# Half of the one-hot matrices on ScalarE, one joint inverse root, a shorter ELU, mixer columns from DRAM and the bias at an eviction

## The reference, cut to what matters

```python
def _rgcn_layer(X, W, root, bias, gamma, beta, src, dst, etype, inv_deg):
    h = jnp.einsum('ni,rio->rno', X, W)
    msg = h[etype, src] * inv_deg[:, None]
    agg = jax.ops.segment_sum(msg, dst, num_segments=X.shape[0])
    out = agg + X @ root + bias
    mu = jnp.mean(out, axis=-1, keepdims=True)
    var = jnp.mean(jnp.square(out - mu), axis=-1, keepdims=True)
    out = (out - mu) * jax.lax.rsqrt(var + EPS) * gamma + beta
    out = jax.nn.elu(out)
    return out + X
...
# the mixer beside it (elu(q)+1, elu(k)+1, a sum over all nodes, two layer norms, a gelu layer)
t = jnp.einsum('nlhd,nhmd,nlh->nlhm', q, kv, z)
x1 = layer_norm(t + x, ln1_g, ln1_b)
h = jax.nn.gelu(jnp.einsum('nfc,oc->nfo', x1, W1) + b1, approximate=False)
y = jnp.einsum('nfc,oc->nfo', h, W2) + b2
return layer_norm(y + x1, ln2_g, ln2_b)
```

## Time and profile before

| | us |
|---|---|
| median of 3 runs | 8429.41 (8418.92 to 8451.86) |
| the profiled execution | 8445.94, its span 8444.1 |
| VectorE busy | 4887.0 (58% of the span) |
| TensorE busy | 5985.2 (71%) |
| ScalarE busy | 1584.5 (19%) |
| GpSimd busy | 4238.0 (50%) |

### The profile page before, as it was taken

The page is one execution under the profiler, slowest core; times in us unless marked ns, Lnnn a source line. Parts: engine busy times, 40 slices in busy tenths (PEclk is TensorE's granted clock), DMA queues, the critical chain, the costliest instruction groups (busy, mean ns, idle before and its releaser), DMA issues. The chain is left out here.

```text
span 8444.1 us, 107673 instructions
## 1 busy us (share of the span) xinstructions
PE 5985.2 (71%) x18474; PEld 3592.9 (43%) x18474; DVE 4887.0 (58%) x16836; ACT 1584.5 (19%) x3834; POOL 4238.0 (50%) x4288
## 2 busy tenths in 40 slices
PE   0587777767777767777776777778488677664398
PEld 0244444444544444444443333345334444443265
DVE  7106666667777767777776677732433666662412
ACT  0231112211111113333330000022021111110132
POOL 0007677756666656666656777710000777762211
PEclk9799899988788888889887666679699888877699
DMA  1324444433333333434434333300034333330000
GB/s 54 127 93 124 120 125 124 125 118 113 112 112 114 113 117 114 118 116 119 119 111 127 104 104 104 103 24 0 0 129 138 105 105 105 105 92 2 12 14 17
DMA packets 457906, 797.23 MB, mean 94 GB/s; under 512 B 87260, under 2 KB 322100, under 8 KB 457609
## 3 DMA queue, kind: packets, MB, share of 16 engines
q0 software_dynamic: 200480, 548.02, 22.9%
q1 hardware_dynamic: 257382, 248.75, 8.9%
HBM read 606.70 MB, written 189.74 MB: 94 GB/s over the span
## 5 line engine op out<-in xcount | busy, mean ns | idle before, releaser
L515 POOL DMA_INDIRECT gnn_msg<-tables,gnn_row_ring x4165 | 4015.2, 964 | 2346.5 <-issue 1644.2
L559 PE MATMUL bank<-gnn_msg,gnn_hot 128*128 128x256 f32 x8330 | 3142.9, 496 | 1292.5 <-DVE sums L544 1030.5
L559 PEld LDWEIGHTS bank<-gnn_msg,gnn_hot 128*128 128x128 f32 x8330 | 1715.7, 235 | 2586.6 <-DVE sums L544 1928.3
L544 DVE TENSOR_TENSOR sums<-sums,bank 128x256 f32 x4165 | 1746.5, 419 | 1587.6 <-PE bank L559 1127.2
L524 DVE TENSOR_SCALAR gnn_hot<-iota,gnn_meta_ring 128x128 f32<-128x128 f32 x3332 | 1127.5, 356 | 332.0 <-ACT gnn_meta_ring L508 332.0
L133 POOL TENSOR_TENSOR ve<-mv,eps 128x7 f32<-128x7 f32 x35 | 7.2, 205 | 1348.3 <-DVE mv L127 1199.7
L652 PE MATMUL bank<-gnn_w,residual 128*128 128x512 f32 x1176 | 572.5, 611 | 1.4 <-ACT residual L668 1.4
L507 ACT COPY gnn_row_ring<-row 128x9 int32 (+1 forms) x490 | 97.8, 200 | 1512.7 <-PE bank L559 1498.8
L1698 PE MATMUL bank<-tables_w,sums 128*128 128x512 f32 x784 | 338.3, 593 | 6.4 <-ACTq L117 6.4
L652 PEld LDWEIGHTS bank<-gnn_w,residual 128*128 128x128 f32 x1176 | 237.2, 202 | 174.7 <-issue 152.9
L672 ACT COPY residual<-bank 128x512 f32<-128x512 f32 x294 | 172.3, 586 | 681.3 <-PE bank L652 681.3
(11 more groups left out here) (398 smaller groups left out, 6804.7 us busy)
## 6 DMA issues: line engine op xcount, KB each, us to landing
tables<-residual SPq DMA_DIRECT2D x294, 256.0 KB, 2.7
gnn_msg<-tables,gnn_row_ring POOLq DMA_INDIRECT x4165, 2.8
tables<-sums SPq DMA_DIRECT2D x98, 512.0 KB, 2.9
tables<-gnn_msg SPq DMA_DIRECT2D x98, 256.0 KB, 2.1
residual<-first_norm SPq DMA_DIRECT2D x98, 128.0 KB, 3.1
first_norm<-state SPq DMA_DIRECT2D x1, 6272.0 KB, 20.8
first_rows<-residual SPq DMA_DIRECT2D x1, 6272.0 KB, 39.0
mixer_rows<-residual SPq DMA_DIRECT2D x49, 128.0 KB, 2.4
```

The lines of the kernel that those rows point to most:

```text
L515: self.nc.gpsimd.indirect_dma_start(out=self.msg[:, s0 + u, :], out_offset=None, in_=table, in_offset=bass.IndirectOffsetOnAxis(ap=self.ro ...
L544: self.nc.vector.tensor_tensor(at, at, self.sums(s), ALU.add).then_inc(self.added, 1)
L559: self.nc.tensor.matmul(self.sums(s), self.hot[:, s, :], self.msg[:, s, :], start=True, stop=True).then_inc(self.summed, 1)
```

## The change

Five things are changed in `gnn0` and its helpers, the first one in `gnn1` too.

1. **One-hots.** Of the 9 and 8 one-hots of a tile's halves VectorE makes 5 and 4. The last four of each half are made by ScalarE inside `ring`, right behind the two copies: four distances |place - iota|, a negated copy of the weights, then four max(weight - weight * distance, 0). So `ring` grows by nine instructions on ScalarE, and TensorE waits for these slots on a semaphore of their own.
2. **Joint root.** `Attend` and `Feed` no longer take an inverse root of their own behind their statistics. Their variance stands beside `Post`'s, and the root after slot 1 is taken of both columns at once, with 12 instructions in place of 9. The mixer's shift follows there, and ScalarE's `norm` moves to the start of its turn, ahead of the copy of the turned tile and of `Gelu` or `Exp`. `Keys0` and the fourth layer take the 12-instruction form for one column.
3. **ELU.** exp(min(u, 0)) takes a `Relu` and an `Exp` on ScalarE; VectorE's cut (L617) is gone, and the -1 goes into the addition to the state, which moves from slot 8 to slot 7.
4. **Mixer columns.** In the table stage the turned tiles are stored to DRAM (28 more DMAs); `Keys0` and `Attend` load them and neither transpose nor copy. `Feed` still does.
5. **Bias.** The one-row matmul is gone. VectorE adds the bias when it evicts the root product, in the table stage and after slot 15 of `Post`; ScalarE's copies of it are gone. `Post`'s steps on TensorE move one slot ahead (9, 11, 12, 14).

```diff
-NEXT_HOTS = (((), (0,), (1,), (2,), (3,), (4,), (5,), (6,), (7,)),
-             ((), (), (0, 1), (2,), (3,), (4, 5), (6,), (7, 8)))
+DVE_HOTS = (5, 4)
+ACT_HOTS = 4
+NEXT_HOTS = (((), (), (0,), (), (1,), (), (2,), (), (3,)),
+             ((), (), (0,), (1,), (), (2,), (3,), (4,)))
...
     def ring(self, act, i, n, h):
...
+        for k in range(ACT_HOTS):
+            u = DVE_HOTS[h] + k
+            self.nc.scalar.activation(self.away[:, k, :], self.c.iota[:], ACT.Abs, bias=m[:, u, 0:1], scale=-1.0)\
+                .then_inc(self.away_ready, 1)
+        if self.weighted:
+            self.nc.scalar.mul(m[:, :, 2], m[:, :, 1], -1.0).then_inc(self.away_ready, 1)
...
+        for k in range(ACT_HOTS):
+            u = DVE_HOTS[h] + k
+            to = self.hot[:, s0 + u, :]
+            if self.weighted:
+                ins = self.nc.scalar.activation(to, self.away[:, k, :], ACT.Relu, bias=m[:, u, 1:2], scale=m[:, u, 2:3])
...
     def vector(self, dve, n, t, cols, last=False):
...
-                inverse_root(dve, c, self.rs, self.half, self.tmp, self.mv[:, 1:2], self.s_root, n - 1)
+                inverse_root(dve, c, self.rs[:, 0:cols], self.half[:, 0:cols], self.tmp[:, 0:cols], self.mv[:, 0:cols, 1],
+                             self.s_root, n - 1)
...
             if s == 6:
                 dve.wait_ge(self.s_exp, n)
-                v.tensor_scalar(self.ex, self.ex, 1.0, -1.0, ALU.min, ALU.add).then_inc(self.s_cut, 1)
+                v.scalar_tensor_tensor(self.u, self.u, 0.0, self.ex, ALU.max, ALU.add).then_inc(self.s_elu, 1)
             if s == 7:
-                dve.wait_ge(self.s_cut, n)
-                v.scalar_tensor_tensor(self.u, self.u, 0.0, self.ex, ALU.max, ALU.add).then_inc(self.s_elu, 1)
-            if s == 8:
                 dve.wait_ge(self.s_elu, n)
...
-                    v.tensor_tensor(self.xs, state, self.u, ALU.add).then_inc(self.s_new, 1)
+                    v.scalar_tensor_tensor(self.xs, self.u, -1.0, state, ALU.add, ALU.add).then_inc(self.s_new, 1)
+            if s == 15 and not last:
+                dve.wait_ge(self.s_prod, n * 3)
+                v.tensor_tensor(agg, c.bank[1][:, 0:D], self.vecs[:, 2, :], ALU.add).then_inc(self.s_base, 1)
...
-        self.nc.scalar.activation(self.ex, self.u, ACT.Exp).then_inc(self.s_exp, 1)
+        self.nc.scalar.activation(self.ex, self.u, ACT.Relu, scale=-1.0).then_inc(self.s_neg, 1)
+        act.wait_ge(self.s_neg, n)
+        gate(act, self.c)
+        self.nc.scalar.activation(self.ex, self.ex, ACT.Exp, scale=-1.0).then_inc(self.s_exp, 1)
...
     def end_first(self, dve, i):
...
-        inverse_root(dve, c, self.rs, self.ve, self.tmp, self.mv[:, 1:2], self.s_pow, i)
-        v.scalar_tensor_tensor(self.shift, self.mv[:, 0:1], -1.0, self.rs, ALU.mult, ALU.mult).then_inc(self.s_rs, 1)
+
+    def shift_mean(self, dve):
+        self.nc.vector.scalar_tensor_tensor(self.shift, self.mv[:, 0:1], -1.0, self.rs, ALU.mult, ALU.mult).then_inc(self.s_rs, 1)
...
     def sync(self, sp, i, first, second):
         if first:
-            sp.wait_ge(self.s_turned, i + 1)
-            sp.dma_start(self.x, self.c.xn_d[ds(i * P, P), :]).then_inc(self.s_x, 16)
+            sp.wait_ge(self.s_mm, i + 1)
+            sp.dma_start(self.xt.rearrange("p h r -> p (h r)"), tile_columns(self.c, i)).then_inc(self.s_xt, 16)
...
-                            if j == 2:
-                                ins = nc.tensor.matmul(c.bank[b][:, 0:D], c.ones[0:1, :], brow[:], start=False, stop=True)
...
-                        nc.scalar.copy(tile_of(c.agg, g, k), c.bank[b][:, 0:D]).then_inc(s_root, 1)
...
+                with dve.Fori(0, NG) as g:
+                    for k in range(GT):
+                        b, t = turn(3 * k + 2, g)
+                        dve.wait_ge(c.bank_full[b], t)
+                        nc.vector.tensor_tensor(tile_of(c.agg, g, k), c.bank[b][:, 0:D], vecs[:, 2, :], ALU.add).then_inc(s_root, 1)
```

More of the change, by code:

```diff
@@ L531, in begin_vector @@
         dve.wait_ge(self.ring_ready, n * 4 + 2)
-        for u in range(HALF):
+        for u in range(DVE_HOTS[0]):
             self.one_hot(0, u)
@@ L932, in after @@
         def after(s):
-            if s == 6 and first:
+            if s == 1 and second:
+                self.shift_mean(dve)
+            if s == 5 and first:
                 dve.wait_ge(self.s_act, i * 2 + 3)
@@ L1029, in scalar @@
         c, sc = self.c, self.nc.scalar
+        if second:
+            self.norm(act, i)
         if first:
```

256 lines of the change are left out of this document (132 added, 124 removed).

## The result

| | us |
|---|---|
| kernel before, 4 runs | 8439.37 (8418.92 to 8451.86) |
| changed kernel, 4 runs | 8295.55 (8290.02 to 8312.18) |
| ratio | 0.9835 [0.9809, 0.9862] |
| profiled execution after | 8290.0, its span 8288.2 |

The change gained 144 us. The prediction said 324 (8105 us, range 7900 to 8270): right in sign, more than twice too much in size, and the range missed by 26 us.

A forecast was written before the change was run, and what follows sets the result against it. It took VectorE to bound Attend and Feed, TensorE Keys0's second half, and POOL's gathers the fourth layer and gnn1. -152 - 118 - 15 - 39 = -324 us from 8429.4 gave 8105 us, range 7900 to 8270.

The forecast's parts named there:

- Attend, -152: Layer beside Attend: VectorE's work falls 3.1 us a tile, 26.45 to 23.3, over 49 tiles -152 us.
- Feed, -118: Layer beside Feed: -2.85 us a tile on VectorE, +0.45 for ScalarE's order, so -2.4 a tile, -118 us.
- I take +0.45 for this stall and the later additions: Feed's tile: Exp ready at about 10.1 us, VectorE wanting it at 9.4; with later additions, 0.45 us a tile lost.
- Covered, with 1.2 us to spare: Attend's tile: despite the later turned tile, TensorE finishes slot 16 at 19.0 us, before VectorE's addition at 20.2.
- Keys0, -15: Layer beside Keys0: turned tile 1.0 us later, products and bias saving more; -0.3 a tile, -15 us.
- ScalarE's price, 3.3 us a half: ScalarE between ring copies and turned tile: eight instructions at 0.35 us, plus overlap and waits, 3.3 us a half.
- Table stage, -39: Table stage: no bias on TensorE -30 us, no root-product copy on ScalarE -9, stores of turned tiles 0.
- Fourth layer and gnn1, 0: These two layers stand at POOL's floor of back-to-back gathers, so no change, 0 us (-10 to +10).
- Rival 1: First three layers all reach the 21.4 us floor because VectorE's register loads hide: 7792 us, half-way about 7950; chance 0.18.
- Rival 2: ScalarE's chain 1 us longer a half: Keys0 and Feed lose 1 us a tile, Attend 0.5; 8227 us, chance 0.14.
- Rivals 3 and 4: 3: ScalarE between ring and turned tile, slower, 8600 us, chance 0.05. 4: TensorE's lower clock cancels layer savings, 8390, chance 0.05.
- Rival 5: Fewer VectorE one-hots free GpSimd's port in the two floor layers, 266 us more gained: 7839 us, chance 0.02.

The follow-up runs named there:

- norm_behind_c: Changed kernel with Feed's normalisation on ScalarE put back behind the turned tile's copy and Gelu: 8146.65 us, 0.9658 of the kernel before.
- norm_and_split_c: Changed kernel, Feed's normalisation behind copy and Gelu, half 0's ScalarE one-hots in two pieces behind the copy of Post's turned tile: 7982.26 us, 0.9468 of the kernel before.
- paced_vector: Changed kernel with all 17 one-hots on VectorE, POOL writing zeros instead of gathering in the first four layers: 8231 us, against 8285 with ScalarE's one-hots.
- narrow_before: Kernel before with each gather taking 32 numbers a row in place of 256, on a slow chip: 9785 us beside 9784 uncut.
- paced_elu: Changed kernel with the ELU of before, POOL writing zeros instead of gathering in the first four layers, on a slow chip: 8828 us.

## Why the prediction was wrong, point by point

- **Attend, -152:** right, -142, but part of the agreement is luck. The root did what was said: additions 11 and 12 stand 3.23 us apart, predicted 2.9 and before 5.6. The aggregation's wait shows with 0.30, not 0.15:

```profile
2426.40 0.42 DVE L551 TENSOR_TENSOR sums<-sums,bank 128x256 f32 x1 [0.21 <-DVE sums L551]
...
2429.63 0.42 DVE L551 TENSOR_TENSOR sums<-sums,bank 128x256 f32 x1 [0.30 <-DVE gnn_own L834]
```

  A joint step takes 0.59 us (predicted 0.61). One-hots and cut were counted 0.7 us too high (1.5 and 0.2 against 1.0 and 0.0), yet the tile fell by 2.9 of the 3.1, so some other term was too low; which one no run tells. The register loads stayed at 2065 ns in the median.
- **Feed, -118: the step that failed.** "I take +0.45 for this stall and the later additions" was, by the layer's pace, +3.5 (27.43 against 26.82 - 2.85). The chain to Exp had been timed well: Exp ends 10.0 us behind the addition of slot 0 in the mean, forecast 10.1. But the stall was priced at VectorE waiting for Exp, and there VectorE doesn't wait. The same late copy holds TensorE's queue after slot 3, 4.8 us a tile, so the addition of slot 4 comes 8.3 us behind that of slot 0 in place of 6.4, and slots 5 to 8, the ring of half 0 and POOL stand behind it. The queue was named; its price in POOL's wait was not worked out. The order cost 2.9 us a tile (norm_behind_c). The second part of the failure is a term put at nothing: the turned tile that comes later by ScalarE's one-hots was checked against VectorE in Attend ("Covered, with 1.2 us to spare") and isn't in Feed's sum, where its place cost another 1.6 (norm_and_split_c). With both put right Feed takes 22.87, 1.1 us less than 26.82 - 2.85, so the sum also left out a gain; in that run TensorE's granted clock over the layer was 0.97 in place of 0.87.
- **Keys0, -15: failed too,** +25. Its three terms (+1.0, -0.8, -0.62) make -0.42 a tile and not the -0.3 taken; either way the sign was wrong. The rings of the layer's 49 tiles part it. From half 0's ring to half 1's it takes 11.8 us in the mean, 11.7 before: the turned tile that comes 1.1 us later (3.79 against 2.7) ate the credit of 1.42, of which 0.63 shows in one tile (7.76 us from the copy to the next ring, 1307.10 to 1314.86, and 8.39 in the tile of the earlier trace rows). The products no longer stand behind slot 12, but slot 12 now stands behind the first product, VectorE waits there 1.74 us, and the products are slower (665 ns against 617 in this layer; TensorE's granted clock over it was 0.85 in place of 0.92). From half 1's ring to half 0's it takes 12.1 us, 11.5 before: the 0.5 us that the layer lost lie here, and the sum had nothing for this stretch. With the one-hots of half 0 moved the first stretch falls to 10.2 and the second stays near 11.9 (norm_and_split_c); without any one-hot on ScalarE the second is 12.2 (paced_vector). So ScalarE's one-hots don't explain it, and what does stays open.
- **ScalarE's price, 3.3 us a half:** right. The groups of the profile after:

```profile
L512 ACT ACTIVATE gnn_hot<-gnn_away,gnn_meta_ring 128x128 f32<-128x128 f32 x1568 | 645.8, 482 | 47.3 <-ACT gnn_meta_ring L503 0.8
L500 ACT ACTIVATE gnn_away<-iota,gnn_meta_ring 128x128 f32<-128x128 f32 x1960 | 626.0, 390 | 58.1 <-ACT gnn_meta_ring L495 0.3
```

  482 and 390 ns with an overlap of 0.09 us make 2.9 us of the eight, and with negation and waits 3.3 from the end of the ring's copies to the end of the last one-hot (1303.63 to 1306.89 in the tile beside Keys0). The Trainium skill (ScalarE: Activation LUTs, What ACT_TABLE_LOAD costs) gives 280 ns and 0.833 ns a column with one pointer operand, an estimate of 387 ns for 128 columns, and about 93 more for the second; the trace agrees to 3 ns. The 0.35 us taken for each of the eight, overlap taken off, was 0.35 to 0.37.
- **Table stage, -39:** -49, 10 us better. **Fourth layer and gnn1, 0:** right (-4 and -2).
- **Rival 1** (the floor) didn't happen: POOL still waits for the ring. **Rival 2** named the mechanism of Keys0 and Feed, but for a longer ScalarE chain; the chain had the length taken, and what it holds was priced too low. **Rivals 3 and 4** were its stronger forms; slower products as in rival 4 were there beside Keys0 and Feed, what they alone cost was not tried. **Rival 5:** the gathers' median went from 947 to 949 down to 946 ns with half the one-hots, 2 us in a layer. By the port rule of the Trainium skill (SBUF - State Buffer, Who interferes with whom) the prediction's estimate was 266 us in all, which doesn't show; whether VectorE made the one-hots in a two-port mode no trace says.

## What to carry to other kernels

When work moves from a full engine to an idle one, list for each queue that it enters what stands behind it there, and follow the last wait through to the engine that issues the loads; pricing it only at the first engine that notices is most of the 148 us by which Feed missed its forecast. Put moved work behind whatever another engine waits for: in the runs without gathers ScalarE's one-hots went from a loss of 54 us against leaving them out to a gain of 156 when the nine instructions of half 0 stood behind the copy (8285, 8231 and 8075 us), and the same normalisation behind the copy instead of ahead of it gave 144. A sum that agrees (Attend) can still hold terms that are off, so read each from the trace.

## What the runs showed of the hardware

The kernel before, with its gathers as long as ever (946 ns on POOL), ran in 8437 to 8443 us on some chips and in 9784 to 9943 on others. The difference lies in the layers in which POOL gathers by DMA, as idle time for which the profile names no releaser, on VectorE (923.2 us in place of 267.5 ahead of its additions), on TensorE (487.6 in place of 12.4 ahead of the one-hot products) and on ScalarE (342.6 ahead of the first evictions, L672, where the first measurement has none). It doesn't depend on the gathers' bytes (narrow_before) and goes with the gathers (paced_elu, on such a chip). There the change costs 1.1% and the version that gains 5.3% elsewhere 1.6%. What delays the engines there stays open.
